# Gated cross-attention and ternary FFN on one core: two kinds of low half formed by GpSimd instead of VectorE, with new orders

## The reference

```
x = x + tanh(g_xattn) * attention(layernorm(x), ctx, ctx, mask)      # softmax(q k^T / sqrt(32)) v, then Wo
x = x + tanh(g_ffn)   * ffn(layernorm(x))
ffn(z) = bitlinear(silu(bitlinear(z, w_gate)) * bitlinear(z, w_up), w_down)
bitlinear(a, w) = round(a * 127 / max|a|) * ternary(w), scaled back
```

## Time and profile before

| | before |
|---|---|
| median of 3 runs | 1370.9 us (1368.8 to 1372.8) |
| the profiled execution's own time | 1373.2 us |
| its span, first to last instruction | 1371.4 us |
| TensorE busy | 1267.3 us, 92% |
| VectorE busy | 1153.7 us, 84% |
| ScalarE busy | 864.8 us, 63% |
| GpSimd busy | 737.6 us, 54% |
| mean granted TensorE clock | 0.974 of full speed |

### The profile page before, as it was taken

The page is one execution under the profiler, slowest core; times in us unless marked ns, Lnnn a source line. Parts: engine busy times, 40 slices in busy tenths (PEclk is TensorE's granted clock), DMA queues, the critical chain, the costliest instruction groups (busy, mean ns, idle before and its releaser), DMA issues.

```text
span 1371.4 us, 26005 instructions
## 1 busy us (share of the span) xinstructions
PE 1267.3 (92%) x7424; PEld 632.0 (46%) x7998; DVE 1153.7 (84%) x2641; ACT 864.8 (63%) x1340; POOL 737.6 (54%) x1187
## 2 busy tenths in 40 slices
PE   5747799999999999999999999999999999998996
PEld 2223344545454454545454454545445454544542
DVE  6967698897979799897979799797979889795884
ACT  2785656658584766758575765758475665856653
POOL 2131654557475564657365564657466465755562
PEclk9868899999999999999999999999999999999999
DMA  9795347464564647365564646455463746453233
GB/s 311 212 239 128 85 86 169 100 154 112 134 138 107 146 107 173 99 151 119 128 146 97 158 108 156 108 143 128 112 155 93 176 107 146 109 139 86 73 83 81
DMA packets 386617, 181.64 MB, mean 132 GB/s; under 512 B 324147, under 2 KB 357811, under 8 KB 384947
## 3 DMA queue, kind: packets, MB, share of 16 engines
q1 hardware_dynamic: 386560, 181.04, 54.6%
HBM read 61.64 MB, written 35.46 MB: 71 GB/s over the span
## 4 chain that ended last, share of the span: by engine, by line
PE 59%; DVE 28%; DMA 4%; issue 4%; ACT 4%; POOL 1%; SPq 1%; POOLq 0%; ACTq 0%; DVEq 0%
PE bank L1198 20%; PE bank L1210 16%; PE bank L1141 5%; DVE region L1009 5%; DVE nmax L948 4%; PE bank L1068 4%; PE bank L1070 4%; PE bank L1069 4%; DVE xh L938 3%; DVE xbig L976 2%; DVE xn L933 2%; DVE hmx L1015 2%; DVE st L980 2%; DMA region<-hb 2%; PE bank L1114 1%
## 5 line engine op out<-in xcount | busy, mean ns | idle before, releaser
L607 POOL TENSOR_TENSOR region<-region,up 128x512 f32<-128x512 f32 x256 | 344.9, 1350 | 135.1 <-DVE region L1009 84.6
L1198 PE MATMUL bank<-tern_gate,region 128*128 128x512 fp8e4 x1024 | 265.1, 382 | 1.2 <-DVE o L1037 1.0
L1198 PE MATMUL bank<-tern_up,region 128*128 128x512 fp8e4 x1024 | 264.4, 381 | 0.0
L1210 PE MATMUL bank<-tern_down,region 128*128 128x512 fp8e4 x1024 | 233.2, 382 | 12.2 <-DMA region<-hb 11.5
L739 ACT ACTIVATE region<-bank,fs 128x512 f32<-128x512 f32 x256 | 177.4, 697 | 92.1 <-PE bank L1198 91.7
L1009 DVE SCALAR_TENSOR_TENSOR region<-region,bank 128x512 f32<-128x512 f32 x256 | 173.4, 682 | 62.4 <-ACT region L739 57.5
L1015 DVE TENSOR_REDUCE hmx<-region 128x1 f32<-128x512 f32 x256 | 170.7, 678 | 57.1 <-POOL region L607 56.8
L598 POOL TENSOR_TENSOR work<-work 124x512 f16<-124x512 f32 x160 | 193.0, 1229 | 40.0 <-ACT work L708 32.9
L563 POOL TENSOR_TENSOR rs<-mv,lnc 128x1 f32<-128x1 f32 (+1 forms) x80 | 26.5, 331 | 292.8 <-DVE mv L983 283.0
L747 ACT ACTIVATE up<-bank 128x512 f32<-128x512 f32 x256 | 152.5, 611 | 13.9 <-PE bank L1198 13.1
L752 ACT ACTIVATE hb<-region 128x2048 bf16<-128x2048 f32 x64 | 122.7, 1918 | 52.7 <-DVE region L1031 52.7
(11 more groups left out here) (142 smaller groups left out, 2455.9 us busy)
## 6 DMA issues: line engine op xcount, KB each, us to landing
q_stack<-q_rows SPq DMA_DIRECT2D x96, 256.0 KB, 4.9
xbig<-in_x SPq DMA_DIRECT2D x16, 1024.0 KB, 5.3
q_rows<-q SPq DMA_DIRECT2D x64, 256.0 KB, 2.0
out_y<-o SPq DMA_DIRECT2D x64, 256.0 KB, 3.1
q_stack<-mT SPq DMA_DIRECT2D x32, 256.0 KB, 4.1
region<-in_wgT SPq DMA_DIRECT2D x4, 1024.0 KB, 12.7
region<-in_wuT SPq DMA_DIRECT2D x4, 1024.0 KB, 5.1
region<-in_wdT SPq DMA_DIRECT2D x4, 1024.0 KB, 5.6
```

The lines of the kernel that those rows point to most:

```text
L607: nc.gpsimd.tensor_tensor(ht, ht, up[:, n % 2, :], ALU.mult).then_inc(hmul_ready, 1)
L1198: ins = T.matmul(pb[2 * (n % 2) + w][:, :], xqT[:, k, tok], tern[w][:, k * FF + n * GT:k * FF + (n + 1) * GT], start=(k == 0), stop=(k == ...
L1210: ins = T.matmul(pb[2][:, :], hT[:, t % 2, k, :], tern[2][:, k * GT:(k + 1) * GT], start=(k == 0), stop=(k == FK - 1))
```

## The change

`x_low` and `a_low` are moved, as they are, from VectorE's program to GpSimd's. Each read its inputs on VectorE after an instruction of VectorE's own; now VectorE can run ahead of them, so two waits are added there: `norm_tile` waits for xl two tiles back in every group (before, only from the third tile on), and `normalise` waits for al two tiles back before it writes at32. The order strings of all five engines are new in all three stages. The diff is shown with the strings of the looped turn, with GpSimd's first string and with parts of VectorE's first one.

```diff
--- before.py
+++ after.py
 TENSOR_ORDER = """
-    F:gu00 F:gu01 F:gu02 A:sc00 A:sc01 F:gu03 A:sc02 F:gu10 A:sc03 A:sc04 E:down30 A:sc10 A:sc11 A:pv00 A:pv01
-    A:sc12 F:gu11 A:sc13 A:sc14 A:pv02 A:pv03 F:gu12 F:gu13 A:pv10 A:pv11 F:gu20 A:pv12 F:down00 A:pv13 A:wo00
-    F:gu21 A:wo10 F:gu22 A:wo20 F:gu23 Q:q00 Q:q10 Q:q20 Q:q30 A:wo30 Q:s00 F:down10 Q:s01 F:gu30 Q:s10 F:gu31
+    F:gu00 F:gu01 F:gu02 A:sc00 A:sc01 F:gu03 A:sc02 F:gu10 A:sc03 A:sc04 E:down30 A:sc10 A:sc11 F:gu11 A:pv00
+    A:sc12 A:pv01 F:gu12 A:pv02 A:sc13 F:gu13 A:sc14 A:pv03 F:gu20 F:down00 A:pv10 A:pv11 F:gu21 A:pv12 A:pv13
+    F:gu22 F:gu23 A:wo00 A:wo10 A:wo20 Q:q00 Q:q10 Q:q20 Q:q30 A:wo30 Q:s00 F:down10 Q:s01 F:gu30 Q:s10 F:gu31
     Q:s11 F:gu32 Q:s20 F:gu33 Q:s21 Q:s30 Q:s31 F:down20 Q:mT00
 """
 SCALAR_ORDER = """
-    F:gu00 F:up00 E:hb30 F:gu01 F:up01 F:up02 F:gu02 A:sc00 A:sc01 F:gu03 A:sc02 F:gu10 F:up03 A:sc03 A:sc04
-    F:up10 A:sc10 A:sc11 A:sc12 A:ah00 F:gu11 A:ah01 F:up11 A:sc13 A:sc14 F:hb00 F:gu12 A:ah02 F:up12 F:up13
-    A:ah03 F:gu13 F:gu20 A:ah10 A:ah11 A:ah12 N:xh00 N:xh10 A:ah13 F:gu21 F:up20 N:xh20 N:xh30 F:gu22 F:up21
-    F:gu23 F:up22 Q:q00 F:up23 Q:q10 F:hb10 A:zq00 A:zb00 Q:q20 Q:q30 F:hb20 A:zq10 A:zb10 A:zq20 F:gu30 F:up30
-    F:gu31 F:up31 F:gu32 F:up32 F:gu33 A:zb20 F:up33 A:zq30 A:zb30 Q:mT00
+    F:gu00 F:up00 E:hb30 F:gu01 F:up01 F:gu02 A:sc00 F:up02 A:sc01 F:gu03 A:sc02 F:up03 F:up10 F:gu10 A:sc03
+    A:sc04 A:sc10 A:sc11 F:up11 F:gu11 A:sc12 A:ah00 F:gu12 F:hb00 A:ah01 F:up12 F:gu13 F:up13 A:sc13 A:ah02
+    F:gu20 A:sc14 A:ah03 N:xh00 F:up20 A:ah10 N:xh10 F:gu21 F:up21 A:ah11 N:xh20 A:ah12 F:gu22 N:xh30 A:ah13
+    F:gu23 F:hb10 F:up22 Q:q00 F:up23 Q:q10 Q:q20 A:zq00 Q:q30 A:zq10 A:zb00 F:hb20 A:zb10 F:gu30 F:gu31 F:up30
+    F:gu32 A:zq20 F:up31 F:gu33 A:zb20 F:up32 F:up33 A:zq30 Q:mT00 A:zb30
 """
 VECTOR_ORDER = """
-    E:hq30 F:gu00 F:gu01 F:hm00 F:gu02 F:hm01 F:hm02 F:gu03 F:hm03 F:gu10 F:hs00 E:down30 F:hq00 A:pv00 A:pv01
-    A:al00 F:gu11 A:al01 A:pv02 A:pv03 N:ln00 F:gu12 A:al02 A:pv10 A:al03 F:gu13 A:pv11 F:hm10 A:al10 A:pv12
-    F:hm11 A:al11 F:down00 N:xn00 N:xn10 A:al12 N:xl00 N:xl10 N:xn20 A:pv13 N:xn30 F:hm12 A:wo00 F:gu20 F:gu21
-    N:xl20 A:st00 N:xl30 A:al13 A:wo10 A:st10 F:gu22 F:hm13 A:wo20 A:zn00 F:gu23 A:st20 F:hs10 F:hq10 Q:q00
-    F:hm20 A:za00 A:zn10 Q:q10 A:za10 F:hm21 F:hm22 F:hm23 Q:q20 F:hs20 Q:q30 F:hq20 A:zn20 A:wo30 Q:s00 A:st30
-    A:za20 Q:s01 F:down10 F:gu30 A:zn30 Q:s10 F:gu31 Q:s11 F:hm30 F:gu32 Q:s20 F:hm31 F:gu33 Q:s21 Q:s30 F:hm32
-    A:za30 Q:s31 F:hm33 Q:mh00 F:hs30 F:down20
+    E:hq30 F:gu00 F:gu01 F:gu02 F:hm00 F:hm01 F:hm02 F:gu03 F:hm03 F:gu10 F:hs00 E:down30 F:hq00 A:pv00 F:hm10
+    F:gu11 A:pv01 F:gu12 N:ln00 A:pv02 F:gu13 N:xn00 A:pv03 F:gu20 F:down00 F:hm11 A:pv10 A:pv11 N:xn10 F:gu21
+    F:hm12 N:xn20 N:xn30 A:pv12 F:hm13 A:pv13 F:hs10 A:wo00 A:st00 F:hq10 F:hm20 A:wo10 A:st10 F:gu22 A:zn00
+    F:gu23 F:hm21 A:za00 A:wo20 Q:q00 A:st20 Q:q10 F:hm22 A:zn10 F:hm23 A:za10 Q:q20 F:hs20 F:hq20 Q:q30 A:zn20
+    A:wo30 Q:s00 A:st30 A:za20 F:down10 Q:s01 A:zn30 F:gu30 Q:s10 A:za30 Q:s11 F:gu31 F:hm30 Q:s20 F:gu32 F:gu33
+    Q:s21 Q:s30 F:hm31 Q:s31 F:hm32 Q:mh00 F:hm33 F:hs30 F:down20
 """
 POOL_ORDER = """
-    F:gu00 F:gu01 F:gu02 A:sc00 A:sc01 A:sc02 F:gu03 A:sc03 A:sc04 A:sc10 A:sc11 F:gu10 A:sc12 A:sc13 A:sc14
-    F:gu11 F:gu12 N:l100 F:gu13 A:l200 F:gu20 F:gu21 A:l210 F:gu22 F:gu23 A:l220 A:l230 F:gu30 A:l300 A:l310
-    F:gu31 F:gu32 F:gu33 A:l320 A:l330
+    F:gu00 F:gu01 F:gu02 A:sc00 A:sc01 F:gu03 A:sc02 A:sc03 A:sc04 F:gu10 A:sc10 A:sc11 A:al00 A:sc12 F:gu11
+    A:al01 N:l100 A:sc13 A:sc14 A:al02 F:gu12 A:al03 N:xl00 F:gu13 A:al10 N:xl10 A:al11 F:gu20 A:al12 N:xl20
+    N:xl30 F:gu21 A:l200 A:l210 A:al13 F:gu22 F:gu23 A:l300 A:l220 A:l230 F:gu30 A:l310 F:gu31 F:gu32 A:l320
+    F:gu33 A:l330
 """
 SYNC_ORDER = """
-    E:tH30 A:x00 A:ta00 A:ta01 F:tH00 A:ta02 A:ta03 A:ta10 A:ta11 A:ta12 N:tx00 N:tx10 N:tx20 N:tx30 A:ta13
-    Q:qd00 F:tH10 A:vl00 A:kv10 Q:qd10 A:vl10 Q:qd20 E:down30 Q:qd30 A:vl20 F:tH20 F:down00 A:vl30 Q:qs00 A:tz00
-    A:tz10 Q:qs10 F:down10 A:tz20 A:vl40 Q:kv00 A:tz30 Q:m00 F:down20
+    E:tH30 A:x00 A:ta00 F:tH00 A:kv10 A:ta01 A:ta02 A:ta03 N:tx00 A:ta10 N:tx10 A:ta11 A:ta12 A:vl00 N:tx20
+    N:tx30 E:down30 F:tH10 A:ta13 Q:qd00 Q:qd10 A:tz00 Q:qd20 F:down00 A:vl10 F:down10 F:tH20 A:tz10 Q:qs00
+    A:vl20 A:vl30 Q:qd30 A:tz20 Q:kv00 Q:qs10 Q:m00 F:down20 A:tz30 A:vl40
 """
...
 POOL_FIRST = """
-    M:l100 W:wx00 W:kx00 W:wx10 W:vx00 W:wm00 N:l100 W:wm10 A:sc00 A:sc01 A:sc02 A:sc03 A:sc04 A:sc10 A:sc11
-    A:sc12 A:sc13 A:sc14 W:wm20 A:l200 A:l210 A:l220 A:l230 A:l300 A:l310 A:l320 A:l330
+    M:l100 M:xl00 M:xl10 W:wx00 M:xl20 W:kx00 M:xl30 W:wx10 W:vx00 W:wm00 N:l100 W:wm10 N:xl00 A:sc00 A:sc01
+    A:sc02 A:sc03 A:sc04 A:al00 A:al01 A:sc10 A:sc11 A:al02 A:sc12 A:sc13 A:al03 A:sc14 N:xl10 A:al10 A:al11
+    N:xl20 W:wm20 N:xl30 A:al12 A:al13 A:l200 A:l210 A:l220 A:l300 A:l230 A:l310 A:l320 A:l330
 """
...
 VECTOR_FIRST = """
-    W:hc00 M:ln00 W:hd00 M:xn00 M:xn10 M:xl00 M:xn20 M:xl10 W:wx00 M:xn30 N:ln00 W:wp00 M:xl20 M:xl30 W:km00
-    W:wx10 W:kp00 W:wl00 W:kc00 W:wp10 W:vm00 R:q00 W:wm00 R:q10 W:wu00 W:wu01 W:wc00 W:wu02 R:q20 R:q30 W:wc01
...
+    W:wp10 W:vm00 R:q00 W:wm00 R:q10 W:wu00 R:q20 W:wu01 W:wc00 R:q30 W:wu02 W:wc01 R:s00 W:wc02 R:s01 W:wu03
+    R:s10 W:wc03 R:s11 W:vp00 R:s20 R:s21 R:s30 W:wl10 R:s31 R:mh00 W:es00 N:xn00 N:xn10 W:vc00 W:wm10 W:wu10
...
@@ -606,7 +605,16 @@
                 pool.wait_ge(up_ready, k)
                 nc.gpsimd.tensor_tensor(ht, ht, up[:, n % 2, :], ALU.mult).then_inc(hmul_ready, 1)
 
-            pieces = {"A": {"sc": p_low, "l2": ln2, "l3": ffn_scales}, "N": {"l1": ln1}, "F": {"gu": h_product},
+            def x_low(g, t, _):
+                pool.wait_ge(xh_ready, g * TT + (t + 1))
+                nc.gpsimd.tensor_tensor(xh[:, t % 2, 1, :], xn[:, t % 2, :], xh[:, t % 2, 0, :], ALU.subtract).then_inc(xl_ready, 1)
+
+            def a_low(g, hf, t):
+                at = TT * hf + t
+                pool.wait_ge(ah_ready, g * (2 * TT) + (at + 1))
+                nc.gpsimd.tensor_tensor(ah[:, at % 2, 1, :], at32[:, at % 2, :], ah[:, at % 2, 0, :], ALU.subtract).then_inc(al_ready, 1)
+
+            pieces = {"A": {"sc": p_low, "al": a_low, "l2": ln2, "l3": ffn_scales}, "N": {"l1": ln1, "xl": x_low}, "F": {"gu": h_product},
                       "W": {"wx": projection_max, "kx": key_max, "vx": value_max, "wm": weight_sum}}
             pieces["M"], pieces["R"] = pieces["N"], pieces.get("Q")
             pieces["E"] = pieces["G"] = pieces["H"] = pieces["I"] = pieces["F"]
@@ -928,14 +936,10 @@
             def norm_tile(g, t, _):
                 if t == 0:
                     dve.wait_ge(ln1_rstd, g + 1)
-                if t >= 2:
+                if g or t >= 2:
                     dve.wait_ge(xl_ready, g * TT + (t - 1))
                 V.tensor_scalar(xn[:, t % 2, :], x_tile(g, t), mv1[:, t, 0:1], rs1[:, 1, t:t + 1],
                                 ALU.subtract, ALU.mult).then_inc(xn_ready, 1)
-
-            def x_low(g, t, _):
-                dve.wait_ge(xh_ready, g * TT + (t + 1))
-                V.tensor_tensor(xh[:, t % 2, 1, :], xn[:, t % 2, :], xh[:, t % 2, 0, :], ALU.subtract).then_inc(xl_ready, 1)
 
             def q_low(g, cc, _):
                 dve.wait_ge(q_hi_ready, g * KC + (cc + 1))
@@ -963,13 +967,10 @@
                 dve.wait_ge(pv_mm, g * (2 * TT) + (at + 1))
                 src = pb[6 + at % 2][:, 0:HH * HW].rearrange("p (h n) -> p h n", h=HH)
                 step(V.reciprocal(rcp[:, t % 2, :], src[:, :, DH]), g * DS + (2 + at))
+                if g or at >= 2:
+                    dve.wait_ge(al_ready, g * (2 * TT) + (at - 1))
                 V.tensor_tensor(at32[:, at % 2, :].rearrange("p (h d) -> p h d", h=HH), src[:, :, 0:DH],
                                 rcp[:, t % 2, :].unsqueeze(2).to_broadcast([P, HH, DH]), ALU.mult).then_inc(norm_ready, 1)
-
-            def a_low(g, hf, t):
-                at = TT * hf + t
-                dve.wait_ge(ah_ready, g * (2 * TT) + (at + 1))
-                V.tensor_tensor(ah[:, at % 2, 1, :], at32[:, at % 2, :], ah[:, at % 2, 0, :], ALU.subtract).then_inc(al_ready, 1)
 
             def residual(g, t, _):
                 dve.wait_ge(wo_mm, g * TT + (t + 1))
@@ -1038,9 +1039,9 @@
                                        ALU.mult, ALU.add).then_inc(out_ready, 1)
 
             pieces = {"Q": {"q": q_low, "s": s_max, "mh": m_split},
-                      "A": {"pv": normalise, "al": a_low,
+                      "A": {"pv": normalise,
                             "wo": residual, "st": ln2_tile, "zn": z_norm_tile, "za": z_amax},
-                      "N": {"ln": ln1, "xn": norm_tile, "xl": x_low},
+                      "N": {"ln": ln1, "xn": norm_tile},
                       "F": {"gu": gu, "hm": h_amax, "hs": h_scale, "hq": hq, "down": output},
```

84 lines of the change are left out of this document (41 added, 43 removed).

## The result

The changed kernel takes 1405.8 us in the median of four runs (1405.6 to 1408.4), the kernel before took 1371.5 us beside it; the ratio is 1.0257, with an interval of 1.0237 to 1.0277. The forecast was 1364.6, with 1384 as the upper end. It was wrong in sign, and no rival gave this time. The profiled execution took 1405.95 us, its span is 1404.1.

The account below looks back on a forecast made before the run. TensorE bounds the kernel, losing time to VectorE's order at two places, not its load. Terms -6.9 - 0.4 + 1 + 0 = -6.3 us took the median 1370.9 to 1364.6; own range 1359 to 1367, overall 1352 to 1384.

Parts of the forecast that it names:

- The first turn: From the start to the second mT: set-up, v's last chunk, late p_low and q00 sum to +1 us, bounds -4 to +5.
- The set-up: Before the first mT: wx10 moves ahead and fits, value matmuls start sooner; -1.7 us, bounds -3.5 to 0.
- v's last chunk: First turn: issued ahead of a 1 MB weight load, easing pv00's 3.15 us wait; -1 us, bounds -2.5 to 0.
- The late p_low: First turn: GpSimd's al00 to al03 delay the last p_low, sc14, to near 104 us; +4.9 us.
- q00: First turn: weaker coupling of q00 to the last at32 gives back 1.2 us.
- The middle: Looped turns: 0.53 us less per period, -6.9 us over 13 periods, and -0.4 in the second turn.
- The gain of 0.78 at q20: Looped turn: q00's low half comes earlier on VectorE, so TensorE's q20 stops waiting; 0.78 us a period, bounds 0 to 0.78.
- The new loss: Looped turn: thin slacks at five late places cost TensorE 0.25 us a period, bounds 0 to 1.6.
- place (c): Looped turn: gu11, at 15.8 us, needs the output of E:down30, expected at 15.5, so covered.
- Places (a), (b), (d) and (e): Looped turn: pv10 needing p_low, down00 hb00, wo00 al10, q00 xl30; each taken as covered, with thin slack.
- the slower rival: Looped turns: GpSimd's stretched p_low chain makes pv10 1.5 us late each period; 1381 us, or 1389; chance 0.25.
- The last turn: End of the kernel: same waits, no subtractions in the closing 50 us; 0, bounds -2 to +3 us.

Follow-up runs that it names:

- s13: Changed kernel with the set-up of the kernel before, group 0's x_low on VectorE there; 1386.5 us (1.0119).
- s1: Kernel before with one spare 128x4 addition on GpSimd between the reductions kx00 and wx10; 1393.1 us (1.0158).
- s3: Changed kernel with GpSimd's set-up reductions put together, behind group 0's x_low; 1393.1 us (1.0169).
- s17: s16 with first-turn al00 and al01 behind the p_low of sc13 and sc14; 1377.9 us (0.9945, on a chip where before mostly took 1382 to 1387).
- s16: s14 with four first-turn low halves (xl20, xl30, al12, al13) put back on VectorE; 1379.2 us (1.0061).
- s12: Kernel before with q00's low half between hs10 and hq10 in VectorE's looped order; 1376.2 us (1.0046).
- s15: s12 with q10's low half also moved, ahead of za00 and zn10; 1378.4 us (1.0073).
- s7: Changed kernel with SyncE's looped kv00 moved behind qs10 and m00; 1401.0 us (1.0216).
- s2: Kernel before with a spare 128x4 addition on GpSimd beside l1's small operations, ahead of the first reduction; 1371.2 us (1.0003).
- s14: s13 with first-turn sc14 sooner: its exponentials ahead of ternary-weight steps, its p_low ahead of al02 and al03; 1387.5 us (1.0135).

## Why the prediction was wrong

**The step that failed is "The first turn".** It had -1.7 - 1.0 + 4.9 - 1.2 = +1, with -4 to +5 as bounds; measured were +29. Term by term:
- The set-up, "wx10 (2.3 us) moves ahead instead and fits", -1.7: it became +16 between the two profiled executions, 19 by the medians of s13 and the changed kernel. I counted x_low at 1.16 us and did not look at what stands between an element-wise operation and a reduction. Moving x_low between the reductions added four changes of 6 to 8.6 us; s1 shows one pair alone, s3 takes two pairs out and gives 12.2 of the 16 back, s13 all. The value matmuls did not even start sooner (27.61 against 27.85): they waited 5.31 us for VectorE's line 836.
- v's last chunk, -1: its wait of 3.15 us is gone, as forecast.
- The late p_low, +4.9: right in mechanism and size at its place, 8.80 against 3.56, so +5.2; behind al00 and al01 moved back (s17) it is 3.5. But s17 shows that taking it out wins nothing by itself, since wo00 waits next.
- q00, -1.2: it had waited 1.6 us and was to wait less; it waited 11.5. What was missing again is a change of kind, at the reduction wm20 in the middle of GpSimd's low halves; without low halves behind it (s16) the turn is 10.9 us shorter.
The bounds failed as well, because they came from durations and none from a gap in front of an instruction. The row with [6.87 <-issue] lay in the trace of before, at 56 us, between the rows 12 of 28 and 93 us.

**The middle, -6.9 and -0.4: measured +4 over 14 turns.** This step failed too, in one term of its sum. The gain of 0.78 at q20 came. The new order is a part of it; whether the lighter VectorE, which the prediction called worth nothing by itself, is another, s12 and s15 suggest and do not show. The new loss, taken at 0.25 a period, was 0.8 (0.87 by the one turn of s7 without it), at place (c): the output was due at 15.5 against 15.8, and ended at 16.6. The collision behind it, a 128x1 operation beside p_low at 1.19 us, is of the kind that the earlier trace rows showed for hs10; I had asked for it only where the old order had it. Places (a), (b), (d) and (e) held in the plain turns, so the slower rival was wrong in its place (no p_low wait in the loop) though not in its kind. Of the operations that the subtractions were to hold on VectorE, xn was held (0.54 to 0.91 us) and hq a little (1.28 to 1.43), z was not, and none of the three is what TensorE waits for in a plain turn.
- The three turns in which the batch changes: not in the prediction. SyncE's kv00, which waits for the last maxima, was put ahead of qs10 and m00; s7 measures it at 4.8 us. It is one word moved past two others in one queue, and I had not followed that queue to its end.
- The terms of the period given as 75.0 us add up to 74.5, so 3.2 us of a period are lost and not 2.7, and 13 periods could give 42 us at most, not 35. The forecast does not use either.

**The last turn**, 0 with bounds -2 to +3: -0.7.

**The chances.** Slower had 0.25 by a mechanism that did not occur. A cost that no rival names cannot have a chance; the first turn should have had one, as it is where most words of the order changed.

## What to carry to other kernels

Before work is put on GpSimd, list its instructions in order by kind, and count every change between element-wise work and a partition reduction at the gap that the trace shows, 5.7 to 10.5 us here, against 1 us for the work itself; keep reductions together and nothing urgent behind them. Where an order has slacks of a few tenths, the gain of a freed place goes to the next one in line, and one collision of 1 us, repeated in each turn, decides the sign: test the loop and the first turn apart. A first turn of a tenth of the time can hold nine tenths of the loss.

## What was not expected of the hardware

The same loop has more than one steady phase: s1 kept a period of 78.8 where before and s2 had 77.7, with only the set-up different. The kernel before itself took 1382 to 1387 us in seven of eight runs on one chip and 1371.9 in the other, and 1379.6 and 1381.6 in two of thirty-two runs on another; whether that is the same second phase stays open, since none of the slower ones was profiled. GpSimd's idle time at a change of kind, where nothing else ended it, was 5.7 (s14) to 7.5 us (s16) in front of a reduction and 6.7 (changed) to 10.5 (s7) behind it. The size of the operation does not tell: an addition of 0.19 us had 7.0 in front of it, an x_low of 1.14 had 7.1. A 128x1 operation of VectorE that started 0.01 us ahead of a p_low took 1.19 us, one that started 0.02 us ahead took 0.15: a hundredth of a microsecond decided over 0.87 us of a turn.
